# Gate half of the projection after the experts, bias and skip seeded into PSUM by ScalarE, and 64-row matmuls in pairs

## The chip, the cores and the metric

The kernel runs on one core of a Trainium2 chip. The metric is the time of one execution on the device in microseconds (us), median of several runs.

## The reference, cut to what matters

Two branches read the same layer-normed `xn` (4 sequences of 4096 tokens, 512 features, float32). The first is a recurrence over every second token, the second a mixture of experts on all tokens; their product is added to the input.

```python
xn = _layernorm(x)
# branch 1, on every second token
x_sub = xn[:, ::2]; x_sub = x_sub * rsqrt(mean(x_sub**2) + 1e-6) * g_norm
x_proj, gate = split(x_sub @ w_in.T + b_in)              # 2 x 512 columns
h = tanh(h * A + xt[:, :, None] * Bm)                    # scan over tokens, h: (4, 512, 64)
y = h @ Cm.sum(axis=0) + Dv * xt
s = repeat((y * silu(gate)) @ w_out.T + b_out, 2)
# branch 2, on all tokens
cont = sigmoid(xn @ W_enc + b_enc) @ W_s2c + b_s2c       # 512 -> 1024 -> 64
gate8 = top-2 of softmax(cont @ Wr + br), renormalised   # 8 experts
expert_out = sum_e gate8[e] * (relu(cont @ W1[e] + b1[e]) @ W2[e] + b2[e])   # 64 -> 512 -> 64
decoded = sigmoid(expert_out @ W_c2s + b_c2s) @ W_dec + b_dec                # 64 -> 1024 -> 512
g = silu(layernorm(decoded))
out = x + s * g
```

## The kernel before, in words

The 2048 steps of the recurrence are cut into 64 blocks of 32 steps; a block carries 128 kept tokens (32 steps of 4 sequences) and the 128 tokens beside them, so 256 tokens for the second branch. The state `h` lies as 128 partitions (4 sequences x 32 of the 64 states) by two halves `f` of 512 features. Of every step GpSimd makes `u = xt * B` (line 513), VectorE multiplies `h` by `A` into PSUM for both halves (line 1068) and adds `u` (line 1074), and ScalarE takes the tanh of each half (line 586). This is a loop of VectorE and ScalarE that no other engine can shorten. `h` is a ring of 8 steps. TensorE reads it four steps at a time (`y`, line 833): group `y(k)` needs the tanhs of steps 4k to 4k+3, and the tanh of step 4k+8 waits until it is done.

All other work of the block before, the block itself and the block after is woven between these steps. Each engine runs its instructions strictly in the order of hand-set "slots", the constants of lines 62 to 113: slot 10.875 of `ACT_SCALE_CONT` puts the work after the second half of step 10, slots of 32 and over fall into the next block, negative ones into the block before. TensorE has no steps of its own, so its slots give only an order. Its order in one period is: end of the experts, `y(4)`, `to_spikes` (line 954: expert output, 64 wide, to 1024 spikes; the output lies as two partial sums on 128 rows and `w_c2s` stands there twice) around `y(5)`, `decode` (971), `y(6)`, `encode` (866), `fin_transpose` (983), `controller` (878: 1024 to 64), `y(0)`, `router` (887), `fin_out` (991), `proj_transpose` (844), `y(1)`, both halves of `proj_in` (853: x_proj and gate), transposes of the scaled controller output (904), `y(2)`, and the experts (918 up, 930 down) with `y(3)` among them.

Two PSUM banks, `bank[0]` and `bank[1]`, are filled in turn by TensorE, 34 fills a block (the `FILL_` constants), and each fill waits until its bank was drained. ScalarE drains most: `spikes` (632), `contT_copy` (655), `scale_cont` (668), `relu` (685), `eo_copy` (689), the seeds of the decoder (697), `proj_evac` (622). VectorE drains `proj_in` with scale and bias (line 1083, into `xp` and `gt`), adds the skip `Dv * x` to `y` (`fin_y`, 1137), routes (1093 to 1111), scales and shifts the decoder's output (1119, 1128) and multiplies the branches (`fin_mul`, 1143, 1144). GpSimd makes the skip product (541), the gate product (546) and the last sum (555). ScalarE applies silu to `gt` in place (627).

Of the kernel before, what the change touches and what calls it, by code (L numbers as in the profile page):

```python
# [26 lines left out]
P = 128  # L27
# [29 lines left out]
FILL_ENC, FILL_FIN, FILL_XT, FILL_WIN, FILL_CONTE, FILL_W1, FILL_C2S, FILL_DEC = 0, 4, 6, 8, 10, 14, 30, 33  # L57
# [9 lines left out]
POOL_PROJ_SCALE = -22.9375  # L67
POOL_DEC_SCALE = (32.5625, 34.1875)
POOL_FIN_SKIP = 25.875
POOL_FIN_GATE = 36.0625  # L70
POOL_FIN_ADD = (49.25, 62.625)
ACT_PROJ_NORM = -23.375
ACT_PROJ_EVAC = (-23.125, -22.4375)
ACT_GATE_SILU = -5.5
ACT_SPIKES = (2.9375, 3.5, 4.625, 5.9375)
# [4 lines left out]
ACT_GATET_COPY = 13.625  # L80
# [22 lines left out]
PE_TO_SPIKES = (33.625, 34.3125, 35.9375, 36.5)  # L103
PE_DECODE = (36.625, 37.0625)
PE_FIN_TRANSPOSE = 53.0
PE_FIN_OUT = 54.4375
DVE_PROJ_EVAC = (-20.1875, -19.4375)
DVE_ROUTE = (8.5, 8.875, 9.125, 9.25, 9.25, 9.5)
DVE_ROUTE_GATE = 10.9375
DVE_DEC_SCALE = (32.75, 36.875)  # L110
DVE_DEC_SHIFT = (33.75, 37.8125)
DVE_FIN_Y = 35.75
DVE_FIN_MUL = 41.9375


def build(nc, x, w_inT, b_in, A_T, B_T, Cm, Dv, w_outT, b_out, g_norm, W_enc, b_enc, W_s2c, b_s2c,
# [12 lines left out]
    with ExitStack() as ctx:  # L129
# [70 lines left out]
        eoT = hT[:, 0, 0:T2]  # L200
        squares_p = hT[:, 0, 0:D]
# [58 lines left out]
        gate_opened = sem("gate_opened")  # L260
# [27 lines left out]
        def fill_number(blk, k):  # L288

            if isinstance(blk, int) and blk == 0:  # L290
                return 4 + k - (2 if k >= FILL_XT else 0)
            if isinstance(blk, int) and blk == LAST:
                return NFILL * blk + 2 + k - (4 if k >= FILL_CONTE else 0)
            return NFILL * blk + 2 + k
# [7 lines left out]
        def proj_fill(blk, k):  # L302

            if isinstance(blk, int) and blk == 0:
                return None, (k - FILL_XT if k < FILL_WIN else 2 + k - FILL_WIN)
            return blk - 1, k
# [75 lines left out]
        def _(sp):  # L382
# [27 lines left out]
            def store_scratch(blk, par):  # L410
                wait_drained(sp, proj_fill(blk, FILL_WIN))
# [78 lines left out]
        def _(pool):  # L490
# [748 lines left out]
```

## Time and profile before

| | |
|---|---|
| median of 3 runs | 5846.17 us (5845.11 to 5853.07) |
| the profiled execution | 5857.5 us, its span 5855.7 us |
| blocks | 64, one every 89.8 us in the middle of the span |
| busy share of the span | TensorE 96%, VectorE 95%, GpSimd 90%, ScalarE 75% |
| granted TensorE clock | 0.993 of full on the mean |

The span runs from the first to the last instruction. Busy time is the time in which an engine had at least one instruction in flight; consecutive instructions overlap a little, so that a sum of durations is more than the time they take, and start-to-start distances are used for costs. A name like `L1068` is line 1068 of the kernel.

### The profile page before, as it was taken

The page shows a single profiled execution, that of the slowest core. Times are in us where ns is not written, and L with a number is a line of the kernel's source. Part 1 is how long each engine was busy: PE and PEld are TensorE (multiplying, and loading weights), DVE is VectorE, ACT ScalarE, POOL GpSimd, SP SyncE. Part 2 cuts the span into 40 slices and gives each one's busy share as a digit, 9 for nine tenths or more (in the row PEclk, how much of TensorE's full clock was granted, in tenths as well). Part 3 has the DMA queues.
Part 4 walks back from the last instruction along what each step waited for, and adds up shares of the span by engine and source line. Part 5 has one row for each costly group of instructions (what it writes and reads, how often), then busy time and mean ns, then how long its engine had stood idle before and what let it go on. Part 6 is the DMA issues. An engine that isn't in the chain of part 4 may idle for free.

```text
span 5855.7 us, 87473 instructions
## 1 busy us (share of the span) xinstructions
PE 5645.0 (96%) x28512; PEld 3153.8 (54%) x28512; DVE 5534.8 (95%) x9300; ACT 4379.6 (75%) x9557; POOL 5298.1 (90%) x2828
## 2 busy tenths in 40 slices
PE   6999999999999999999999999999999999999998
PEld 3555555555555555555555555555555555555554
DVE  5999999999999999999999999999999999999998
ACT  5777777777777777777777777777777777777775
POOL 5999999999999999999999999999999999999897
PEclk9999999999999999999999999999999999999999
DMA  6444444444544445444444444444444444444443
GB/s 162 112 121 107 121 112 112 115 109 116 122 106 121 113 112 123 109 116 120 107 119 116 110 119 110 116 119 106 120 114 112 119 110 116 119 110 115 113 111 89
DMA packets 158218, 673.36 MB, mean 115 GB/s; under 512 B 45761, under 2 KB 46785, under 8 KB 92225
## 3 DMA queue, kind: packets, MB, share of 16 engines
q1 hardware_dynamic: 157762, 667.76, 47.5%
q8 instruction: 227, 3.72, 0.3%
q14 instruction: 229, 1.88, 0.1%
HBM read 617.26 MB, written 50.33 MB: 114 GB/s over the span
## 4 chain that ended last, share of the span: by engine, by line
PE 39%; DVE 33%; ACT 13%; issue 10%; POOL 4%; SPq 1%; DMA 0%; POOLq 0%; DVEq 0%; ACTq 0%
PE bank L918 16%; DVE ps_z L1074 15%; DVE ps_z L1068 13%; ACT h L586 8%; PE bank L853 7%; PE ps_acc L930 7%; PE ps_y L833 4%; POOL u L513 3%; PE bank L904 2%; ACT wide L632 2%; ACT xbuf L616 2%; DVE g L1128 1%; POOL p_root L518 1%; DVE gt L1083 1%; DVE g L1143 1%
## 5 line engine op out<-in xcount | busy, mean ns | idle before, releaser
L513 POOL TENSOR_TENSOR u<-xb,bt 128x1024 f32<-128x1024 f32 x2048 | 4807.9, 2366 | 479.5 <-DVE ps_z L1074 424.0
L586 ACT ACTIVATE h<-ps_z 128x512 f32<-128x512 f32 x4096 | 2421.8, 600 | 1104.8 <-DVE ps_z L1074 1087.4
L1068 DVE TENSOR_TENSOR ps_z<-h,ps_A 128x512 f32<-128x512 f32 x4096 | 2678.1, 692 | 214.3 <-ACT h L586 129.9
L1074 DVE TENSOR_TENSOR ps_z<-ps_z,u 128x512 f32<-128x512 f32 x4096 | 2660.6, 691 | 0.2 <-issue 0.2
L918 PE MATMUL bank<-wide,w 65*128 65x256 f32 x4096 | 1029.9, 396 | 0.0
L833 PE MATMUL ps_y<-h,c_wide 128*32 128x512 f32 x8192 | 978.1, 601 | 0.0
L866 PE MATMUL bank<-xnT,w_enc 128*128 128x256 f32 x4096 | 904.3, 381 | 2.9 <-ACT wide L632 2.9
L918 PEld LDWEIGHTS bank<-wide,w 65*128 65x128 f32 x4096 | 723.4, 190 | 312.0 <-issue 152.7
L866 PEld LDWEIGHTS bank<-xnT,w_enc 128*128 128x128 f32 x4096 | 775.1, 190 | 160.0 <-issue 53.3
L833 PEld LDWEIGHTS ps_y<-h,c_wide 128*32 128x32 f32 x8192 | 221.0, 109 | 515.0 <-issue 443.8
L853 PE MATMUL bank<-w_in,xnT 128*128 128x512 f32 x1024 | 452.9, 595 | 1.6 <-DVE c_wide L1160 1.6
L971 PE MATMUL bank<-w_dec,wide 128*128 128x512 f32 x1024 | 452.6, 595 | 0.0
L971 PE MATMUL ps_acc<-w_dec,wide 128*128 128x512 f32 x1024 | 449.9, 592 | 0.0
L685 ACT ACTIVATE conte<-bank 128x512 f32<-128x512 f32 x512 | 308.3, 602 | 103.0 <-PE bank L918 96.4
L685 ACT ACTIVATE hT<-bank 128x512 f32<-128x512 f32 x512 | 298.4, 597 | 89.3 <-PE bank L918 87.8
L971 PEld LDWEIGHTS ps_acc<-w_dec,wide 128*128 128x128 f32 x1024 | 194.6, 190 | 244.9 <-issue 244.9
L971 PEld LDWEIGHTS bank<-w_dec,wide 128*128 128x128 f32 x1024 | 189.0, 189 | 225.9 <-issue 166.5
L853 PEld LDWEIGHTS bank<-w_in,xnT 128*128 128x128 f32 x1024 | 190.6, 191 | 218.0 <-issue 215.9
L930 PE MATMUL ps_acc<-conte,w 128*64 128x256 f32 x2048 | 281.1, 395 | 0.0
L930 PE MATMUL ps_acc<-hT,w 128*64 128x256 f32 x2048 | 279.8, 394 | 0.0
L991 PE MATMUL bank<-w_out,conte 128*128 128x512 f32 x512 | 236.7, 605 | 19.8 <-ACT bank L710 19.8
L668 ACT ACTIVATE conte<-ps_acc,gate 128x64 f32<-128x64 f32 x1024 | 228.5, 379 | 0.0
(118 smaller groups left out, 4264.2 us busy)
## 6 DMA issues: line engine op xcount, KB each, us to landing
xb<-x_proj_scratch SPq DMA_DIRECT2D x2048, 256.0 KB, 4.5
xbuf<-in_L_attn_x SPq DMA_DIRECT2D x256, 128.0 KB
xres<-in_L_attn_x SPq DMA_DIRECT2D x512, 64.0 KB
out<-g SPq DMA_DIRECT2D x256, 128.0 KB
x_proj_scratch<-xp SPq DMA_DIRECT2D x256, 64.0 KB
w_in<-in_L_attn_w_in SPq DMA_DIRECT2D x1, 2048.0 KB, 8.3
w_enc<-in_L_ffn_W_enc SPq DMA_DIRECT2D x1, 2048.0 KB, 16.6
w_dec<-in_L_ffn_W_dec SPq DMA_DIRECT2D x1, 2048.0 KB, 20.2
```

What stands on the lines that cost most here:

```text
L513: pool.tensor_tensor(u[:, tau % 2, :, :], xt, bt[:, :, :], ALU.mult).then_inc(u_ready, 1)
L586: act.activation(h[:, tau % RING, f, :], ps_z[:, f, :], ACT.Tanh).then_inc(h_ready, 1)
L685: drained(act.activation(hidden[n % 4], bank[n % 2][:, :], ACT.Relu), at)
L833: ins = pe.matmul(ps_y[32 * j:32 * j + 32, :], c_wide[:, f, SP - 4 - 4 * k:2 * SP - 4 - 4 * k], h[:, (QUAD * k + j) % RING, f, :], start=( ...
L853: ins = pe.matmul(bank[half][:, :], xnT[:, par, k, 0, :], w_in[:, k, D * half:D * half + D], start=(k == 0), stop=(k == KD - 1))
L866: ins = pe.matmul(bank[n % 2][:, T2 * half:T2 * half + T2], w_enc[:, k, P * m:P * m + P], xnT[:, par, k, :, :], start=(k == 0 and half == ...
L918: ins = pe.matmul(bank[n % 2][:, T2 * half:T2 * half + T2], w_1[0:MA, e, P * t:P * t + P], conteT[:, e, :], start=True, stop=True)
L930: ins = pe.matmul(eo_acc[M * half:M * half + M, :], w_2[:, 4 * (n // 2) + t, :], hidden[n % 4][:, T2 * half:T2 * half + T2], start=(n == 0 ...
L971: ins = pe.matmul(dst[:, :], wide[:, k, P * q:P * q + P], w_dec[:, k, :], start=False, stop=(k == KH - 1), skip_group_check=True)
L991: ins = pe.matmul(bank[1][:, :], oT[:, k, :], w_out[:, k, :], start=False, stop=(k == KD - 1), skip_group_check=True)
L1068: dve.tensor_tensor(ps_z[:, f, :], h[:, (tau - 1) % RING, f, :], ps_A[:, f, :], ALU.mult).then_inc(m_done, 1)
L1074: dve.tensor_tensor(ps_z[:, f, :], ps_z[:, f, :], u[:, tau % 2, f, :], ALU.add).then_inc(z_ready, 1)
```

## The change

- **Gate's projection.** `proj_in` of the gate half leaves its place beside the x_proj half and runs after the experts of the block before (slot 4.625), as fill 29, ahead of the spikes' fills. The fill numbers of the expert work alternate anew, so that each bank sees the same order as before.
- **Bias by seed.** ScalarE writes `b_in` divided by the row's scale into the bank (`proj_seed`), the matmuls add onto it, and ScalarE drains with the row's scale (`proj_out`): a copy to `xp` for the first half, a silu straight into `gt` for the second. VectorE's two `proj_evac` and the silu in place are gone.
- **Skip by seed.** GpSimd multiplies `xp` by `Dv` in place once `xp` is stored (`fin_skip`, slot 0.4375, before at 25.875), ScalarE copies it into `ps_y` (`y_seed`), the `y` matmuls add onto it, and ScalarE copies the sum out (`fin_y`). VectorE's `fin_y` is gone.
- **Spikes in pairs.** Two matmuls (`eo_fold`) add the two partial sums of the expert output and put the result on both halves of the partitions; ScalarE copies it (`both_copy`); `to_spikes` then takes 64 rows for each matmul, two row halves in turn, into different banks, in two calls in place of four.
- **Controller.** `controller` waits for each pair of spike tiles before the matmuls that read it, and not for all of them first.
- The slots of all engines are set anew, and a few small operations of the scale are made in other forms.

```diff
-FILL_ENC, FILL_FIN, FILL_XT, FILL_WIN, FILL_CONTE, FILL_W1, FILL_C2S, FILL_DEC = 0, 4, 6, 8, 10, 14, 30, 33
+FILL_ENC, FILL_FIN, FILL_XT, FILL_IN, FILL_GATE, FILL_C2S, FILL_DEC = 0, 4, 6, 8, 29, 30, 33
+FILL_CONTE = (10, 9, 12, 11)
+FILL_W1 = (14, 13, 16, 15, 18, 17, 20, 19, 22, 21, 24, 23, 26, 25, 28, 27)
+FILL_WIN = (FILL_IN, FILL_GATE)
...
-POOL_PROJ_SCALE = -22.9375
-POOL_DEC_SCALE = (32.5625, 34.1875)
-POOL_FIN_SKIP = 25.875
...
-ACT_PROJ_NORM = -23.375
-ACT_PROJ_EVAC = (-23.125, -22.4375)
-ACT_GATE_SILU = -5.5
...
-ACT_CONTT_COPY = 6.6875
-ACT_ROUTE_SIG = 8.875
-ACT_SCALE_CONT = (10.875, 11.75)
-ACT_CONTET_COPY = (12.125, 12.5, 12.9375, 13.5)
...
-ACT_RELU = (13.625, 14.4375, 14.6875, 15.0, 16.75, 16.8125, 17.75, 17.8125, 18.6875, 19.6875, 19.9375, 20.0, 20.625, 21.5, 21.9375, 22.9375)
-ACT_EO_COPY = 23.6875
-ACT_SPIKES_AGAIN = (24.5, 24.9375, 26.625, 27.5625)
...
-ACT_DEC_SEED = (25.8125, 27.625)
-PE_Y = (22.3125, 22.5625, 24.0625, 26.75, 33.125, 34.375, 38.375, 45.25)
-PE_PROJ_TRANSPOSE = (-9.5625, -9.4375)
-PE_PROJ_IN = (-9.375, -9.3125)
-PE_ENCODE = (16.3125, 16.3125, 17.0, 18.4375)
-PE_CONTROLLER = 21.8125
-PE_ROUTER = 22.3125
-PE_CONTET = (22.8125, 23.75, 23.875, 24.6875)
-PE_GATET = 24.5625
-PE_EXPERTS = (25.125, 25.125, 26.3125, 27.5625, 28.4375, 29.0625, 30.0, 30.3125, 32.0)
...
-DVE_PROJ_EVAC = (-20.1875, -19.4375)
-DVE_ROUTE = (8.5, 8.875, 9.125, 9.25, 9.25, 9.5)
...
-DVE_FIN_Y = 35.75
...
+POOL_FIN_SKIP = 0.4375
...
+ACT_PROJ_NORM = -23.4375
+ACT_PROJ_EVAC = (-22.6875, -20.25)
+ACT_PROJ_SEED = (-22.3125, -9.125)
+ACT_PROJ_OUT = (-20.4375, -7.25)
+ACT_FIN_Y = 33.8125
+ACT_Y_SEED = 5.625
+ACT_SPIKES = (2.9375, 3.8125, 4.6875, 5.875)
+ACT_CONTT_COPY = 6.8125
+ACT_ROUTE_SIG = 9.5
...
+ACT_RELU = (13.375, 13.875, 14.5625, 14.75, 15.5, 15.5625, 16.5625, 16.5625, 17.8125, 17.8125, 18.8125, 20.9375, 21.625, 21.875, 22.6875, 22.8125)
+ACT_EO_COPY = 23.625
+ACT_BOTH_COPY = 24.875
+ACT_SPIKES_AGAIN = (25.75, 25.9375, 26.625, 27.75)
...
+ACT_DEC_SEED = (26.3125, 27.875)
+PE_Y = (19.1875, 20.375, 21.5, 34.8125, 34.9375, 37.25, 38.125, 38.375)
+PE_PROJ_TRANSPOSE = (-12.0, -10.625)
+PE_PROJ_IN = (-11.5625, 4.625)
+PE_ENCODE = (6.4375, 7.1875, 7.3125, 11.1875)
+PE_CONTROLLER = 17.125
+PE_ROUTER = 19.0625
+PE_CONTET = (22.0, 26.3125, 27.4375, 28.0)
+PE_GATET = 21.4375
+PE_EXPERTS = (28.9375, 33.3125, 34.0, 34.125, 34.4375, 34.4375, 35.5625, 35.9375, 36.25)
...
+PE_EO_FOLD = 36.75
+PE_TO_SPIKES = (36.9375, 37.3125)
+PE_DECODE = (37.4375, 37.8125)
...
+PE_FIN_TRANSPOSE = 50.8125
+PE_FIN_OUT = 51.25
...
+DVE_ROUTE = (7.75, 8.75, 9.375, 9.5, 9.625, 9.75)
+DVE_ROUTE_GATE = 10.0
...
@@ -257,7 +266,10 @@
         p_moments = sem("p_moments")
         p_scale_steps = sem("p_scale_steps")
         p_normed = sem("p_normed")
-        gate_opened = sem("gate_opened")
+        proj_seeded = sem("proj_seeded")
+        y_seeded = sem("y_seeded")
+        eo_folded = sem("eo_folded")
+        both_copied = sem("both_copied")
         contT_ready = sem("contT_ready")
         contT_copied = sem("contT_copied")
...
@@ -515,13 +527,13 @@
             def proj_scale(blk):
 
                 pool.wait_ge(p_moments, blk + 1)
-                pool.tensor_tensor(p_root[:, :, :], p_var[:, :, :], minus_half[:, :].rearrange("p (n q) -> p n q", n=2),
-                                   ALU.pow).then_inc(p_scale_steps, 1)
+                pool.tensor_tensor(p_root[:, 0:3], p_var[:, 0:3], minus_half[:, 0:3], ALU.pow).then_inc(p_scale_steps, 1)
                 pool.wait_ge(p_scale_steps, 4 * blk + 1)
-                pool.tensor_tensor(p_nm[:, :], p_mean[:, :], p_root[:, 0, :], ALU.mult).then_inc(p_scale_steps, 1)
-                pool.tensor_tensor(p_rr[:, :], p_var[:, 0, :], p_root[:, 0, :], ALU.mult).then_inc(p_scale_steps, 1)
+                pool.tensor_tensor(p_nm[:, :], p_mean[:, :], p_root[:, 0:2], ALU.mult).then_inc(p_scale_steps, 1)
+                pool.tensor_tensor(p_both[:, :], p_root[:, 0:1], p_root[:, 2:3], ALU.mult).then_inc(p_scale_steps, 1)
                 pool.wait_ge(p_scale_steps, 4 * blk + 3)
-                pool.tensor_tensor(p_rr[:, :], p_rr[:, :], p_root[:, 1, :], ALU.mult).then_inc(p_scale_steps, 1)
+                pool.tensor_tensor(p_rr[:, :], p_var[:, 0:4:2], p_both[:, :].to_broadcast([P, 2]),
+                                   ALU.mult).then_inc(p_scale_steps, 1)
 
...
                     pool.wait_ge(late_loaded, LATE)
-                pool.wait_ge(eo_ready, blk + 1)
-                pool.tensor_tensor(o, xp[:, par, :], dv_all[:, :], ALU.mult).then_inc(t1_ready, 1)
+                pool.wait_ge(scratch_stored, 16 * QUAD * (blk + 1))
+                pool.tensor_tensor(xp[:, par, :], xp[:, par, :], dv_all[:, :], ALU.mult).then_inc(t1_ready, 1)
 
             def fin_gate(blk, par):
-                pool.wait_ge(gate_opened, blk + 1)
+                wait_drained(pool, proj_fill(blk, FILL_GATE))
                 pool.wait_ge(y_taken, blk + 1)
                 pool.tensor_tensor(o, o, gt[:, par, :], ALU.mult).then_inc(o_ready, 1)
...
                 drained(act.activation(xnT[:, par, :, q, :],
                                        bank[q][:, :].rearrange("p (k t) -> p k t", k=KD), ACT.Copy), at)
 
-            def gate_silu(blk, par):
-                wait_drained(act, proj_fill(blk, FILL_WIN + 1))
-                act.activation(gt[:, par, :], gt[:, par, :], ACT.Silu).then_inc(gate_opened, 1)
+            def proj_seed(blk, half):
+
+                wait_free(act, proj_fill(blk, FILL_WIN[half]))
+                act.wait_ge(p_scale_steps, 4 * blk + 4)
+                act.activation(bank[half][:, :], b_in_all[:, D * half:D * half + D], ACT.Copy,
+                               scale=p_rr[:, 1:2]).then_inc(proj_seeded, 1)
+
+            def proj_out(blk, par, half):
+
+                at = proj_fill(blk, FILL_WIN[half])
+                wait_filled(act, at)
+                if half == 0:
+                    if not (is_first(blk) or blk == 1):
+                        act.wait_ge(y_seeded, blk - 1)
+                    ins = act.activation(xp[:, par, :], bank[0][:, :], ACT.Copy, scale=p_rr[:, 0:1])
+                else:
+                    ins = act.activation(gt[:, par, :], bank[1][:, :], ACT.Silu, scale=p_rr[:, 0:1])
+                drained(ins, at)
+
+            def y_seed(blk, par):
+
+                act.wait_ge(t1_ready, blk + 1)
+                if not is_first(blk):
+                    act.wait_ge(y_taken, blk)
+                act.activation(ps_y[:, :], xp[:, par, :], ACT.Copy).then_inc(y_seeded, 1)
+
+            def fin_y(blk):
+
+                act.wait_ge(y_done, NQ * (blk + 1))
+                act.activation(o, ps_y[:, :], ACT.Copy).then_inc(y_taken, 1)
 
             def half_tanhs(src, k, bias):
...
                 act.activation(eoT, eo_acc, ACT.Copy).then_inc(eo_copied, 1)
+
+            def both_copy(blk):
+                act.wait_ge(eo_folded, blk + 1)
+                act.activation(eoT_both, eo_acc, ACT.Copy).then_inc(both_copied, 1)
 
             def dec_seed(blk, q):
...
@@ -824,16 +880,14 @@
             def y(blk, k):
 
                 pe.wait_ge(h_ready, 2 * STEPS * blk + 2 * QUAD * (k + 1))
-                if k == 0 and is_first(blk):
-                    pe.wait_ge(biases_shifted, 2)
-                elif k == 0:
-                    pe.wait_ge(y_taken, blk)
+                if k == 0:
+                    pe.wait_ge(y_seeded, blk + 1)
                 for f in range(F):
                     for j in range(QUAD):
                         ins = pe.matmul(ps_y[32 * j:32 * j + 32, :],
                                         c_wide[:, f, SP - 4 - 4 * k:2 * SP - 4 - 4 * k],
                                         h[:, (QUAD * k + j) % RING, f, :],
-                                        start=(k == 0 and f == 0), stop=(k == NQ - 1 and f == F - 1))
+                                        start=False, stop=(k == NQ - 1 and f == F - 1), skip_group_check=True)
                 ins.then_inc(y_done, 1)
 
...
             def proj_in(blk, par, half):
 
-                at = proj_fill(blk, FILL_WIN + half)
+                at = proj_fill(blk, FILL_WIN[half])
                 wait_drained(pe, proj_fill(blk, FILL_XT))
-                wait_free(pe, at)
+                pe.wait_ge(proj_seeded, 2 * blk + half + 1)
                 for k in range(KD):
                     ins = pe.matmul(bank[half][:, :], xnT[:, par, k, 0, :], w_in[:, k, D * half:D * half + D],
-                                    start=(k == 0), stop=(k == KD - 1))
+                                    start=False, stop=(k == KD - 1), skip_group_check=True)
                 filled(ins, at)
 
...
             def controller(blk):
 
-                wait_drained(pe, (blk, FILL_ENC + 2))
-                wait_drained(pe, (blk, FILL_ENC + 3))
                 pe.wait_ge(acc_seeded, blk + 1)
                 for k in range(KH):
                     half = k % 2
+                    if half == 0:
+                        wait_drained(pe, (blk, FILL_ENC + k // 2))
                     ins = pe.matmul(contT_acc[M * half:M * half + M, :], w_s2c[:, k, :], wide[:, k, :],
...
@@ -895,7 +950,7 @@
                 ins.then_inc(gateT_ready, 1)
 
             def conteT_transpose(blk, n):
-                at = (blk, FILL_CONTE + n)
+                at = (blk, FILL_CONTE[n])
                 pe.wait_ge(conte_ready, 2 * blk + 2)
                 wait_free(pe, at)
...
@@ -942,21 +997,32 @@
                     expert_down(blk, 2 * p - 2)
                     expert_down(blk, 2 * p - 1)
 
+            def eo_fold(blk):
+
+                pe.wait_ge(eo_copied, blk + 1)
+                for j in range(2):
+                    ins = pe.matmul(eo_acc[M * j:M * j + M, :], halves, eoT, start=True, stop=True)
+                ins.then_inc(eo_folded, 1)
+
             def to_spikes(blk, n):
+
                 if n == 0:
-                    pe.wait_ge(eo_copied, blk + 1)
-                at = None if C2S_FILL[n] is None else (blk, C2S_FILL[n])
-                if at:
-                    wait_free(pe, at)
-                dst = bank[at[1] % 2] if at else ps_acc
+                    pe.wait_ge(both_copied, blk + 1)
+                ats = [None if C2S_FILL[2 * n + j] is None else (blk, C2S_FILL[2 * n + j]) for j in range(2)]
+                for at in ats:
+                    if at:
+                        wait_free(pe, at)
                 for half in range(2):
-                    m = 2 * n + half
-                    ins = pe.matmul(dst[:, T2 * half:T2 * half + T2], w_c2s[:, P * m:P * m + P],
-                                    eoT, start=(half == 0), stop=True, skip_group_check=True)
-                if at:
-                    filled(ins, at)
-                else:
-                    ins.then_inc(acc_filled, 1)
+                    for j in range(2):
+                        dst = bank[ats[j][1] % 2] if ats[j] else ps_acc
+                        m = 2 * (2 * n + j) + half
+                        rows = slice(M * j, M * j + M)
+                        ins = pe.matmul(dst[:, T2 * half:T2 * half + T2], w_c2s[rows, P * m:P * m + P],
+                                        eoT_both[rows, :], start=(half == 0), stop=True, skip_group_check=True)
+                        if half == 1 and ats[j]:
+                            filled(ins, ats[j])
+                        elif half == 1:
+                            ins.then_inc(acc_filled, 1)
 
             def decode(blk, q):
...
@@ -1073,17 +1143,6 @@
                     dve.wait_ge(m_done, t2 + f + 1)
                     dve.tensor_tensor(ps_z[:, f, :], ps_z[:, f, :], u[:, tau % 2, f, :],
                                       ALU.add).then_inc(z_ready, 1)
-
-            def proj_evac(blk, par, half):
-
-                at = proj_fill(blk, FILL_WIN + half)
-                wait_filled(dve, at)
-                dve.wait_ge(p_scale_steps, 4 * blk + 4)
-                dst = (xp, gt)[half]
-                drained(dve.scalar_tensor_tensor(out=dst[:, par, :], in0=bank[half][:, :], scalar=p_rr[:, 0:1],
-                                                 in1=b_in_all[:, D * half:D * half + D],
-                                                 op0=ALU.mult, op1=ALU.add), at)
-
 
             def route(blk, n):
...
@@ -1131,11 +1190,6 @@
                 else:
                     ins.then_inc(acc_drained, 1)
 
-            def fin_y(blk):
-                dve.wait_ge(t1_ready, blk + 1)
-                dve.wait_ge(y_done, NQ * (blk + 1))
-                dve.tensor_tensor(o, ps_y[:, :], o, ALU.add).then_inc(y_taken, 1)
-
             def fin_mul(blk):
```

## Rows read from the trace of the kernel before

**Rows 1.** The page: span, engines, chain that ended last, the recurrence's multiplies.

```profile
span 5855.7 us, 87473 instructions
PE 5645.0 (96%) x28512; PEld 3153.8 (54%) x28512; DVE 5534.8 (95%) x9300; ACT 4379.6 (75%) x9557; POOL 5298.1 (90%) x2828
...
PE 39%; DVE 33%; ACT 13%; issue 10%; POOL 4%; SPq 1%; DMA 0%; POOLq 0%; DVEq 0%; ACTq 0%
...
L1068 DVE TENSOR_TENSOR ps_z<-h,ps_A 128x512 f32<-128x512 f32 x4096 | 2678.1, 692 | 214.3 <-ACT h L586 129.9
```

**Rows 2.** Windows, one period and ten: length, busy PE to POOL, clock, DMA.

```profile
3011.95:3101.75 89.80, 87.57 (x448) 48.99 (x446) 86.30 (x146) 68.24 (x150) 82.79 (x45) 1.00 0.47 115
1000.00:1898.00 898.00, 875.76 (x4427) 489.05 (x4425) 857.97 (x1442) 678.46 (x1478) 824.18 (x439) 0.99 0.48 114
```

**Rows 3.** Timeline of VectorE: start, length, line, tiles, count, [idle before].

```profile
3014.51 1.30 DVE L1068 TENSOR_TENSOR ps_z<-h,ps_A 128x512 f32<-128x512 f32 x2
...
3017.07 1.30 DVE L1068 TENSOR_TENSOR ps_z<-h,ps_A 128x512 f32<-128x512 f32 x2
...
3043.62 1.30 DVE L1068 TENSOR_TENSOR ps_z<-h,ps_A 128x512 f32<-128x512 f32 x2
...
3046.03 0.68 DVE L1137 TENSOR_TENSOR conte<-ps_y,conte 128x512 f32<-128x512 f32 x1
3046.63 1.28 DVE L1068 TENSOR_TENSOR ps_z<-h,ps_A 128x512 f32<-128x512 f32 x2
...
3070.81 1.28 DVE L1068 TENSOR_TENSOR ps_z<-h,ps_A 128x512 f32<-128x512 f32 x2
3072.00 0.69 DVE L1074 TENSOR_TENSOR ps_z<-ps_z,u 128x512 f32<-128x512 f32 x1
3072.96 0.75 DVE L1083 SCALAR_TENSOR_TENSOR gt<-bank,p_rr,b_in_all 128x512 f32<-128x512 f32 x1 [0.27 <-PE bank L853]
...
3074.23 1.45 DVE L1068 TENSOR_TENSOR ps_z<-h,ps_A 128x512 f32<-128x512 f32 x2
```

**Rows 4.** Timeline of TensorE's matmuls, the same period, columns as there.

```profile
3015.40 1.99 PE L954 MATMUL bank<-hT,w_c2s 128*128 128x256 f32 x8
3017.32 1.92 PE L833 MATMUL ps_y<-h,c_wide 128*32 128x512 f32 x16
3019.18 1.13 PE L954 MATMUL ps_acc<-hT,w_c2s 128*128 128x256 f32 x4
...
3021.01 7.07 PE L971 MATMUL bank<-w_dec,wide 128*128 128x512 f32 x16
...
3034.88 3.64 PE L833 MATMUL ps_y<-h,c_wide 128*32 128x512 f32 x32
3038.45 14.08 PE L866 MATMUL bank<-xnT,w_enc 128*128 128x256 f32 x64
...
3054.24 1.95 PE L878 MATMUL ps_acc<-wide,w_s2c 128*64 128x256 f32 x16 [1.28 <-ACT wide L632]
...
3073.86 1.06 PE L904 MATMUL bank<-ident,conte 128*65 128x128 f32 x8 [0.39 <-DVE gt L1083]
...
3082.85 1.99 PE L918 MATMUL bank<-wide,w 65*128 65x256 f32 x8
3084.77 1.08 PE L930 MATMUL ps_acc<-conte,w 128*64 128x256 f32 x8
3085.78 1.93 PE L833 MATMUL ps_y<-h,c_wide 128*32 128x512 f32 x16
```

**Rows 5.** Timeline of ScalarE, three steps, columns as there.

```profile
3016.44 1.20 ACT L586 ACTIVATE h<-ps_z 128x512 f32<-128x512 f32 x2 [1.09 <-DVE ps_z L1074]
3017.53 1.56 ACT L632 ACTIVATE wide<-bank,b_c2s_col 128x256 f32<-128x256 f32 x4
...
3029.24 1.20 ACT L586 ACTIVATE h<-ps_z 128x512 f32<-128x512 f32 x2 [1.36 <-DVE ps_z L1074]
```

**Rows 6.** Groups by line: the expert output's copy; busy us, mean ns.

```profile
L689 ACT ACTIVATE hT<-ps_acc 128x256 f32<-128x256 f32 x64 | 24.2, 377 | 0.0
```

More of the change, by code:

```diff
@@ new lines @@
+ACT_CONTET_COPY = (12.625, 12.75, 12.75, 12.9375)
+ACT_GATET_COPY = 11.6875
+ACT_RELU = (13.375, 13.875, 14.5625, 14.75, 15.5, 15.5625, 16.5625, 16.5625, 17.8125, 17.8125, 18.8125, 20.9375, 21.625, 21.875, 22.6875, 22.8125)
+ACT_EO_COPY = 23.625
+ACT_BOTH_COPY = 24.875
+ACT_SPIKES_AGAIN = (25.75, 25.9375, 26.625, 27.75)
+ACT_DEC_SILU = (31.5, 39.9375)
+ACT_DEC_SQUARE = (29.9375, 31.625)
+ACT_PROJ_SUM = (-29.25, -29.0625)
+ACT_PROJ_MEAN = -28.9375
+ACT_PROJ_SQUARE = (-28.0625, -27.375)
+ACT_PROJ_VAR = -25.0625
@@ new lines @@
+ACT_FIN_EVAC = 39.875
+ACT_ACC_SEED = 5.625
+ACT_OUT_SEED = 38.9375
+ACT_DEC_SEED = (26.3125, 27.875)
[9 more added lines that the diff above has]
+PE_EO_FOLD = 36.75
@@ L200, in build @@
         eoT = hT[:, 0, 0:T2]
+        eoT_both = hT[:, 0, T2:2 * T2]
+        halves = w_r[:, E * E:E * E + M]
         squares_p = hT[:, 0, 0:D]
@@ L292, in fill_number @@
             if isinstance(blk, int) and blk == LAST:
-                return NFILL * blk + 2 + k - (4 if k >= FILL_CONTE else 0)
+                return NFILL * blk + 2 + k - (2 if k > FILL_XT + 1 else 0) - (2 if k > FILL_GATE or k % 2 == 0 and k > FILL_IN else 0)
             return NFILL * blk + 2 + k
@@ L739, in _ @@
             proj_evac(0, 0, 0)
+            proj_seed(0, 0)
             proj_evac(0, 0, 1)
+            proj_seed(0, 1)
+            proj_out(0, 0, 0)
             act.wait_ge(early_loaded, EARLY)
@@ L761, in _ @@
             act.wait_ge(acc_shaped, 1)
+            proj_out(0, 0, 1)
             def between(blk, par, slot):
@@ L778, in between @@
                     proj_var(blk)
-                if slot == ACT_GATE_SILU:
-                    gate_silu(blk, par)
+                for half in range(2):
+                    if slot == ACT_PROJ_SEED[half]:
+                        proj_seed(blk, half)
+                for half in range(2):
+                    if slot == ACT_PROJ_OUT[half]:
+                        proj_out(blk, par, half)
+                if slot == ACT_FIN_Y:
+                    fin_y(blk)
+                if slot == ACT_Y_SEED:
+                    y_seed(blk, par)
                 for k in range(4):
@@ L800, in between @@
                     eo_copy(blk)
+                if slot == ACT_BOTH_COPY:
+                    both_copy(blk)
                 for k in range(4):
@@ L918, in expert_up @@
                     ins = pe.matmul(bank[n % 2][:, T2 * half:T2 * half + T2], w_1[0:MA, e, P * t:P * t + P],
[L919 removed]
+                                    conteT[:, e, :], start=(half == 0), stop=True, skip_group_check=True)
                 filled(ins, at)
@@ L1009, in _ @@
             proj_in(0, 0, 0)
-            proj_in(0, 0, 1)
             pe.wait_ge(weights_shaped, 3)
+            zeros = h[:, RING - 1, 0, :]
+            pe.matmul(ps_y[:, :], zeros[:, 0:P], zeros, start=True, stop=True)
             for k in range(KH):
-                pe.matmul(ps_y[0:M, 0:1], w_s2c[:, k, :], ones[:, 0:1], start=(k == 0), stop=(k == KH - 1))
+                pe.matmul(ps_y[0:M, 0:1], w_s2c[:, k, :], ones[:, 0:1], start=False, stop=(k == KH - 1),
+                          skip_group_check=True)
             for k in range(KH):
@@ L1042, in between @@
                         experts(blk, n)
-                for n in range(4):
+                if slot == PE_EO_FOLD:
+                    eo_fold(blk)
+                for n in range(2):
                     if slot == PE_TO_SPIKES[n]:
@@ L1185, in between @@
             def between(blk, par, slot):
-                for half in range(2):
-                    if slot == DVE_PROJ_EVAC[half]:
-                        proj_evac(blk, par, half)
                 for n in range(6):
@@ L1198, in between @@
                         dec_shift(blk, q)
-                if slot == DVE_FIN_Y:
-                    fin_y(blk)
                 if slot == DVE_FIN_MUL:
```

63 lines of the change are left out of this document (24 added, 39 removed).

## The prediction

> **What bounds the kernel now.** I read the page first, for who is busy at all. TensorE has 96% and VectorE 95% of the span, GpSimd 90%, ScalarE 75%, and the chain that ended last is 39% TensorE and 33% VectorE [rows 1]. So there are two candidates, and neither alone need be the bound. The windows come next, because the kernel repeats itself 64 times: one period takes 89.80 us, and in it TensorE is busy for 87.57, VectorE for 86.30, GpSimd for 82.79 and ScalarE for 68.24. Ten periods give the same shares [rows 2]. The reader should see that TensorE has 2.23 us left in a period.
>
> VectorE's timeline shows what its 86.30 are. A plain step of the recurrence goes from 3014.51 to 3017.07, 2.56 us, four operations and a hand-over to ScalarE and back [rows 3]. 32 of these are 81.9 us, and so 7.9 us of each period are steps made longer, by an operation of VectorE between them or by a tanh that comes late. The second kind costs 129.9 us in all, 2.0 in a period [rows 1]. ScalarE's timeline shows why it can be late: in a plain step it does two tanhs in 1.20 us and is then idle for 1.36, which holds two operations of 512 columns (0.60 each, half of the 1.20) and not three [rows 5]. So TensorE's stream and the loop of VectorE with ScalarE each run at about 98% of the period, tied to each other through the banks, the relus and the ring of `h`. Only a change that takes time from both shortens the period.
>
> **The change part by part.** All sums are for one period, against the profiled execution's own 89.80 us. That execution took 5857.5 us, 11 more than the median of 5846.2, so differences are carried over to the median.
>
> *VectorE.* It loses `fin_y`: the step with it goes from 3043.62 to 3046.63, 3.01 us, 0.45 more than a plain one [rows 3]. It loses the drain of x_proj, an operation of the same kind (0.45), and the drain of the gate half: the step with it goes from 3070.81 to 3074.23, 3.42 us, 0.86 more, of which 0.27 are a wait for the matmuls [rows 3]. Nothing is added. The loop comes to 89.80 - 0.45 - 0.45 - 0.86 = 88.04, if ScalarE is as late as before and not later.
>
> *ScalarE.* It gains two bias seeds, the copy to `xp`, the seed and the drain of `ps_y`, each about 0.60 [rows 5], and `both_copy` at 0.38 as its twin `eo_copy` has [rows 6]; the silu is only moved. That is 3.4 us, and 68.2 + 3.4 = 71.6 of some 88. The free gaps of 32 steps are 32 x 1.36 = 43.5 us, and ScalarE's work beside the tanhs is now 68.2 - 32 x 1.20 = 29.8, after it 33.2. So it fits on the mean, at nothing. If the cover is missing, each operation that is a third one in its gap delays the step by up to 0.5; some places have that (silu, then `both_copy`, just ahead of step 25's tanh; two relus and a seed ahead of step 23). The new waits on ScalarE are for the gate's matmuls before `proj_out`, for the fold before `both_copy`, for the last `y` before `fin_y`, and for GpSimd's product before `y_seed`. The tanhs are queued behind all four, and VectorE waits for the tanhs. By their slots the first two are the ones that matter; the other two have most of a step or more to spare.
>
> *TensorE's work.* `to_spikes` takes 3017.32 - 3015.40 = 1.92 and 3021.01 - 3019.18 = 1.83, together 3.75 us for 16 instructions [rows 4]. The trace has no pair of row halves, but a pair of column halves: eight instructions of line 930, as many columns, take 3085.78 - 3084.77 = 1.01, against 3084.77 - 3082.85 = 1.92 for eight unpaired of line 918 [rows 4]. The bounds for the sixteen are these two paces, 2.02 and 3.75. I take 2.02, because line 930 is the same array cut in half in the other direction. `eo_fold` has four instructions of line 930's form, 0.50. `y(3)` and `y(4)` now stand side by side; 32 such instructions take 3.57 where 16 take 1.86 [rows 4], so this saves 0.15. The work is 87.57 - 3.75 + 2.02 + 0.50 - 0.15 = 86.19.
>
> The 0.15 is also the only price here of changing how the array is cut. The Trainium skill (TensorEngine Tiling (Array Packing), Key Properties) says that changing the tiling mode, not just the tile, drains TensorE, which speaks against this change: around the spikes it has seven such changes where there were five. The trace bears it out at about 0.15 for two changes, one into `y` and one out of it, and the two that `y(4)` no longer needs pay for the new ones, so by the rule the sum stays as it is.
>
> *TensorE's waits.* They are 89.80 - 87.57 = 2.23 now. The wait of the controller for the last spikes is 1.28 [rows 4]. After the change its first 12 of 16 matmuls run ahead of those spikes, 12/16 of the 1.95 us of the row, that is 1.4; but `fin_transpose`, 0.6 us of cover, now stands behind it. 1.28 + 0.6 - 1.4 leaves 0.45, a gain of 0.83. The 0.39 behind the drain of the gate half [rows 4] go, since the drain is off this path. The router now has only `fin_transpose` between it and the controller whose output ScalarE must copy first, where `y(0)` stood, 1.86: the copy (0.38, as in rows 6) and two hand-overs, for which I take 0.25 each as a guess between 0 and 0.5, are about 0.9, less 0.6 of cover, so 0.3; the bounds are 0 and 1.5, with a pair of tanhs in front. The worst new wait is behind the fold: `eo_copy` is hidden behind the gate's matmuls, but after the fold nothing stands between it and `to_spikes`. ScalarE first does the silu (0.60, half of it during the fold), then `both_copy` (0.38), with hand-overs about 1.0. The bounds are 0.7 and 2.2, the upper one with a pair of tanhs in front (1.20) [rows 5]. The seed of the gate half stands behind the last relu, as the last pair of expert matmuls does on TensorE, and both take about as long; I put it at 0, at most 0.6. The waits come to 2.23 - 0.83 - 0.39 + 0.3 + 1.0 = 2.31.
>
> *GpSimd.* The same product is made earlier, in place, with 1.3 us of work moved into the first step and a reciprocal root over three columns in place of four. 82.8 of 88 remain busy; `u` is made up to two steps ahead. I put it at 0; it costs up to 0.5 if `u` comes late in step 1. *SyncE's* queue has the same transfers at the same slots. *The head and the tail* of the span change by less than I can tell.
>
> **Sum.** TensorE's stream is 86.19 + 2.31 = 88.5, the loop of the recurrence 88.04. The larger sets the period: 88.5, a gain of 1.3, and 64 x 1.3 = 83 us. 5846.2 - 83 = 5763 us. Its own range, from the bounds of the waits (period 87.6 to 89.4), is 5705 to 5821.
>
> **The rivals.**
> 1. *Both streams lose their losses.* With less on both sides the late tanhs (2.0) and TensorE's waits may shrink too. TensorE's work is 86.2; with waits of 0.8 the period is 87.0, 64 x 2.8 = 179, 5667 us. For it: every wait of TensorE but the one behind the fold has a cover. Against it: the coupling that makes late tanhs (relus at TensorE's pace of 2.93 us a pair against steps of 2.56) stays.
> 2. *The paired rows do not overlap.* Then the spikes stay at 3.75, and TensorE's stream is 88.5 + 1.73 = 90.2, of which perhaps 0.3 are given back, since the wait behind the fold then has less after it to delay: about 90.0, 13 us more, 5859 us. For it: no row of the trace shows row halves, and the two halves in turn write different banks but through the same columns. Against it: the column pairs of line 930. The Trainium skill (TensorEngine Tiling (Array Packing), Gotcha 1) has row tiles write to different PSUM banks, as the change does; no row here shows that.
> 3. *Slower: ScalarE becomes the late one.* Place: slots 22.7 to 24.9, where seed, silu and `both_copy` join the relus and copies, and where ScalarE stands waiting for the gate's matmuls and then the fold with a tanh behind. Price: six added operations, each the third in its gap, 6 x 0.4 = 2.4 (three operations, 1.80, against the gap of 1.36), plus about 1.0 of standing in the two waits: 88.04 + 3.4 = 91.4, 64 x 1.6 = 102, 5948 us. It decides from 1.8 us of added lateness on (89.80 - 88.04). For it: the gaps hold two operations, and two now come just ahead of a tanh. Against it: ScalarE has 10 us more gap than work.
> 4. *No effect.* The gains are eaten in part, by late tanhs or by a `y` that waits for the ring since TensorE's order around it is new. Period 89.8, 5846 us.
>
> **How the numbers follow.** The forecast has 0.52, rival 1 0.13, rival 2 0.10, rival 3 0.17, rival 4 0.08. The range takes in the forecast's own, most of rival 1 and rivals 2 and 4, and the near part of 3: 5670 to 5880. A measurement of this kernel can tell about 0.2%, 12 us, from no change. Faster: 0.52 + 0.13 and half of what lies around rivals 2 and 4 on that side (0.05), 0.70. Same: 0.09. Slower: 0.17 + 0.04 = 0.21.
>
> **What the profile of after would show.** Right: VectorE's busy time per period near 84.5; eight instructions of `to_spikes` in about 1.0 us; a gap of about 1 us before the first of them; the controller's wait under 0.5; late tanhs still near 2 us a period. Wrong: eight instructions in 1.9 (rival 2); VectorE's idle time before its multiplies, put down to the tanh, over 240 us in all (rival 3); a period below 87.3 (rival 1). What would undo the forecast most easily is the stretch around the fold, where TensorE and ScalarE wait for each other in turn.

## The result, and the profile after

The changed kernel takes 5802.8 us (median of 5 runs, 5799.2 to 5817.2), the kernel before 5853.1 beside it (5 runs); the ratio is 0.9919, with a 95% interval of 0.9896 to 0.9942. That is 50 us less by the medians and 47 by the ratio, which compares the means. It lies inside the range, at a bit over half of the 83 us forecast. The page of the changed kernel (busy times and the chain that ended last, to be held against rows 1), and the window of one period (length, busy times of PE, PEld, DVE, ACT, POOL, granted clock, DMA; against rows 2):

```profile
span 5801.0 us, 88242 instructions
PE 5580.6 (96%) x28770; PEld 3073.1 (53%) x28770; DVE 5403.5 (93%) x9108; ACT 4595.4 (79%) x9941; POOL 5287.9 (91%) x2828
...
PE 76%; ACT 14%; DVE 7%; issue 3%; SPq 1%; DMA 0%; POOL 0%; ACTq 0%; POOLq 0%
...
3009.36:3098.52 89.16, 86.79 (x449) 47.83 (x448) 84.24 (x143) 71.59 (x156) 82.59 (x45) 1.00 0.47 115
```

Work has left VectorE (86.30 to 84.24 in a period) and gone to ScalarE (68.24 to 71.59), as the sum had it. The chain is what changed most: 76% TensorE and 7% VectorE, where it was 39% and 33% [rows 1]. TensorE's timeline over that period, main rows (start, length, line, tiles, count, idle before):

```profile
3012.93 14.08 PE L921 MATMUL bank<-xnT,w_enc 128*128 128x256 f32 x64
3026.95 1.95 PE L933 MATMUL ps_acc<-wide,w_s2c 128*64 128x256 f32 x16
3028.83 0.66 PE L1049 MATMUL bank<-ident,conte 128*128 128x128 f32 x4
3029.38 0.71 PE L942 MATMUL ps_acc<-w_r,hT 128*128 128x128 f32 x4
...
3038.16 3.67 PE L908 MATMUL bank<-w_in,xnT 128*128 128x512 f32 x8
3041.67 0.60 PE L898 MATMUL bank<-ident,xbuf 128*128 128x128 f32 x4
3042.53 0.38 PE L949 MATMUL ps_acc<-ident,gate 128*8 128x128 f32 x2 [0.26 <-ACT conte L707]
3043.69 1.92 PE L887 MATMUL ps_y<-h,c_wide 128*32 128x512 f32 x16 [0.78 <-ACT h L598]
...
3046.97 1.11 PE L959 MATMUL bank<-ident,conte 128*65 128x128 f32 x8 [0.34 <-ACT wide L718]
3048.37 3.90 PE L973 MATMUL bank<-wide,w 65*128 65x256 f32 x16 [0.29 <-ACT wide L718]
...
3075.84 3.70 PE L908 MATMUL bank<-w_in,xnT 128*128 128x512 f32 x8
3079.47 0.65 PE L1004 MATMUL ps_acc<-hT,w_r 128*64 128x256 f32 x4
3080.61 1.14 PE L1020 MATMUL bank<-hT,w_c2s 64*128 64x256 f32 x8 [0.48 <-ACT hT L732]
3081.67 1.92 PE L887 MATMUL ps_y<-h,c_wide 128*32 128x512 f32 x16
```

The controller (L933) and the router (L942) no longer wait at all; the pairs (L1020) take 3081.67 - 3080.61 = 1.06 us for eight. New are a row of four waits around `y(2)`, the third `y` after the encoder, 0.26, 0.78, 0.34 and 0.29, together 1.67, and 0.48 behind the fold. From start to start of the same operations, one period divides so:

| stage on TensorE | before, us | after, us |
|---|---|---|
| y(6), y(7) | 3.57 | 3.57 |
| encoder, up to the controller | 15.79 | 14.02 |
| controller to fin_out | 4.74 | 5.12 |
| fin_out to the first expert | 18.38 | 16.30 |
| experts, up to their end | 25.97 | 27.47 |
| to the decoder (spikes; after: gate, fold, spikes) | 7.49 | 8.75 |
| decoder | 13.87 | 13.93 |
| sum | 89.81 | 89.16 |

The first gain is the controller's wait and `fin_transpose` (which moved one stage on). The fourth stage lost the gate half, about 3.5, and the waits of 0.39 and 0.20 for VectorE, which would make 14.3; it takes 16.3. There the gain was given back.

In both kernels `y(6)` and `y(7)` stand back to back ahead of the encoder. The starts of this doubled `y`, 63 in each trace, give the account of nearly the whole span. Before, 59 of the 62 periods take 89.8 to 89.9 us and three 94.7; after, all 62 take 89.17. In the three long ones the granted clock of TensorE was at half, 1.2 of 2.4 GHz, for some 10 us, as these windows of the kernel before show (length, busy times of PE, PEld, DVE, ACT, POOL, granted clock, DMA share, GB/s):

```profile
1000.00:1011.00 11.00, 10.61 (x58) 5.79 (x56) 10.06 (x17) 9.89 (x25) 8.82 (x4) 1.00 0.24 60
1011.00:1021.60 10.60, 10.60 (x43) 4.71 (x42) 8.85 (x15) 4.83 (x9) 9.55 (x6) 0.53 0.35 71
```

So 64 x (89.80 - 89.17) = 40 and 3 x 4.9 = 15, together 55, which is the difference of the two spans (5855.7 - 5801.0). Between these two executions a quarter of the gain is clock that was no longer lost, and the sum had no term for it. The steady part, 40 us, is a little under half of the 83 forecast.

### The profile page after: what moved, and what is told of

Read it like the earlier page. It is cut to its first block, busy times and chain, and to the rows that moved or that the text cites. A ratio compares the mean times of both kernels' runs of the same rounds, so it can differ in the third digit from the quotient of the medians.

```text
span 5801.0 us, 88242 instructions
## 1 busy us (share of the span) xinstructions
PE 5580.6 (96%) x28770; PEld 3073.1 (53%) x28770; DVE 5403.5 (93%) x9108; ACT 4595.4 (79%) x9941; POOL 5287.9 (91%) x2828
## 3 DMA queue, kind: packets, MB, share of 16 engines
q8 instruction: 229, 3.75, 0.3%
## 4 chain that ended last, share of the span: by engine, by line
PE 76%; ACT 14%; DVE 7%; issue 3%; SPq 1%; DMA 0%; POOL 0%; ACTq 0%; POOLq 0%
PE bank L973 17%; PE bank L921 15%; PE ps_y L887 11%; PE ps_acc L985 9%; PE bank L1037 8%; PE ps_acc L1037 8%; ACT h L598 4%; PE bank L908 4%; DVE ps_z L1144 4%; ACT conte L707 3%; DVE ps_z L1138 2%; ACT wide L718 1%; PE bank L1020 1%; PE ps_acc L1020 1%; PE bank L959 1%
## 5 line engine op out<-in xcount | busy, mean ns | idle before, releaser
L973 PE MATMUL bank<-wide,w 65*128 65x256 f32 x4096 | 1015.0, 393 | 18.5 <-ACT wide L718 18.5
L887 PE MATMUL ps_y<-h,c_wide 128*32 128x512 f32 x8192 | 962.0, 599 | 49.0 <-ACT h L598 49.0
L887 PEld LDWEIGHTS ps_y<-h,c_wide 128*32 128x32 f32 x8192 | 227.2, 109 | 566.8 <-issue 418.1
L908 PE MATMUL bank<-w_in,xnT 128*128 128x512 f32 x1024 | 474.4, 606 | 7.6 <-DVE c_wide L1214 1.6
L724 ACT ACTIVATE conte<-bank 128x512 f32<-128x512 f32 x512 | 291.2, 598 | 24.3 <-PE bank L973 24.3
```

The lines of the kernel that those rows point to most:

```text
L724: drained(act.activation(hidden[n % 4], bank[n % 2][:, :], ACT.Relu), at)
L887: ins = pe.matmul(ps_y[32 * j:32 * j + 32, :], c_wide[:, f, SP - 4 - 4 * k:2 * SP - 4 - 4 * k], h[:, (QUAD * k + j) % RING, f, :], start=F ...
L908: ins = pe.matmul(bank[half][:, :], xnT[:, par, k, 0, :], w_in[:, k, D * half:D * half + D], start=False, stop=(k == KD - 1), skip_group_c ...
L973: ins = pe.matmul(bank[n % 2][:, T2 * half:T2 * half + T2], w_1[0:MA, e, P * t:P * t + P], conteT[:, e, :], start=(half == 0), stop=True, ...
```

## The experiments

All kernels below were timed beside the kernel before; their times are held against 5803 of the changed kernel, "steady period" is the commonest distance between the starts of the doubled `y`. The kernel before had medians of 5856.8, 5857.7 and 5867.3 us in the three rounds of experiments, against 5853.1 beside the changed kernel, so a difference from 5803 is uncertain by up to some 14 us. The steady periods carry the readings.

### Do row halves overlap?

```diff
-                        rows = slice(M * j, M * j + M)
+                        rows = slice(0, M)
```

> The changed kernel, but both matmuls of a pair read rows 0 to 63 instead of one reading 0 to 63 and the other 64 to 127; the same 16 instructions, the same data (it lies on both halves), nothing left out. Theory A (row halves overlap, and TensorE's stream sets the period): eight instructions take about 1.9 us in place of 1.06, twice a period, so 1.7 x 64 = 109 us more than the changed kernel's 5803, about 5912. Rival B (row halves do not overlap, 1.06 is something else): 1.06 stays, 5803. Rival C (they overlap, but the recurrence's loop on VectorE and ScalarE sets the period): eight instructions take 1.9, the time stays within 15 us of 5803.

5914.2 us, ratio 1.0095 (1.008 to 1.011), steady period 90.88.

```profile
3047.40 1.99 PE L1020 MATMUL bank<-hT,w_c2s 64*128 64x256 f32 x8 [0.48 <-ACT hT L732]
3049.32 1.92 PE L887 MATMUL ps_y<-h,c_wide 128*32 128x512 f32 x16
```

Eight matmuls on one row half take 3049.32 - 3047.40 = 1.92 us, on two in turn 1.06. Theory A is right to 2 us: rows overlap, and 1.71 us of TensorE in a period cost 1.71 x 64. In this stretch the stream of TensorE sets the time.

### The spikes as before, in the changed kernel

```diff
-                if slot == ACT_BOTH_COPY:
-                    both_copy(blk)
...
-                    pe.wait_ge(both_copied, blk + 1)
+                    pe.wait_ge(eo_copied, blk + 1)
...
-                        rows = slice(M * j, M * j + M)
+                        rows = slice(0, P)
...
-                                        eoT_both[rows, :], start=(half == 0), ...)
+                                        eoT[rows, :], start=(half == 0), ...)
...
-                if slot == PE_EO_FOLD:
-                    eo_fold(blk)
```

> The changed kernel with the spikes as before: no fold, no second copy, 16 matmuls over 128 rows, in the two calls of the changed kernel. The rest of the change stays. Theory A (TensorE's stream sets the period): the spikes go from 2.12 + 0.66 for the fold + 0.48 of waiting to 3.75, so +0.5 x 64 = 32 us, about 5835. Rival C (the recurrence's loop sets it): ScalarE loses a copy and a wait, 5803 or a little under, 5790.

5887.1 us, ratio 1.0048 (1.0033 to 1.0063): 84 more, where A had 32.

```profile
3037.05 1.97 PE L1018 MATMUL bank<-hT,w_c2s 128*128 128x256 f32 x8 [0.87 <-ACT gt L653]
```

The direction was right and a term was missing: the first spikes go into the bank that the silu drains, and without the fold before them they wait 0.87 us for it. The steady period is 90.47, and 1.30 x 64 = 83. So the fold and its wait cost less than the sum had, since most of that time would otherwise be waiting for the silu.

### The controller all at once, and in pieces in the kernel before

```diff
+                wait_drained(pe, (blk, FILL_ENC + 2))
+                wait_drained(pe, (blk, FILL_ENC + 3))
...
-                    if half == 0:
-                        wait_drained(pe, (blk, FILL_ENC + k // 2))
```

> The changed kernel, but the controller waits for the last two pairs of spike tiles before its first matmul, as in the kernel before. Theory A: 12 of its 16 matmuls no longer run ahead of the last tanhs; a wait of about 1.4 us stands before it in each period, and router, routing and the scaled controller output all come that much later: 64 x 1.4 = 90 us more, about 5890. Rival C: TensorE's wait is covered by the slack of its stream, within 15 us of 5803.

5858.9 us, ratio 1.0002 (0.9993 to 1.0012), steady period 90.00. The wait is 0.98 us, not 1.4; 0.83 of it reach the period, 53 us. (The profiled execution has two periods of 103.1 us besides, with the clock at half for 27 us; more on these below.) The same edit the other way round, in the kernel before:

> The kernel before with one part of the change alone: the controller waits for each pair of spike tiles before the matmuls that read it. In the changed kernel the same edit was worth 56 us when taken away. Theory D (the period is a path in series, on TensorE from the relus to the encoder in the changed kernel, but only between slots 11 and 23 in the kernel before, whose controller stands in the stretch paced by the recurrence): TensorE's wait of 1.28 goes from the controller to the next thing that waits for the recurrence, the time stays, ratio 0.998 to 1.001. If TensorE's stream set the period all along: 0.9 x 64 = 56 us less, ratio 0.990.

5855.3 us beside 5867.3, ratio 0.9980 (0.9971 to 0.9989), steady period 89.80, exactly that of before.

```profile
3061.46 1.95 PE L878 MATMUL ps_acc<-wide,w_s2c 128*64 128x256 f32 x16 [0.47 <-ACT ps_acc L703]
...
3067.00 3.67 PE L991 MATMUL bank<-w_out,conte 128*128 128x512 f32 x8 [0.97 <-ACT bank L710]
```

The controller's wait falls from 1.28 [rows 4] to 0.47, and `fin_out`'s grows from 0.29 to 0.97. One edit is worth 0.83 us a period in one kernel and nothing in the other, since before it stood in a stretch paced by the recurrence. The ratio's 0.2% (12 us) has no steady gain behind it. It goes with the clock: the mean granted clock was 0.992 to 0.996 in the runs of this kernel and 0.990 to 0.993 in those of the kernel before beside it.

### One slot moved

```diff
-PE_Y = (19.1875, 20.375, 21.5, 34.8125, ...
+PE_Y = (19.1875, 20.375, 22.5, 34.8125, ...
```

> The changed kernel with one slot moved: y(2) from 21.5 to 22.5 in TensorE's order, so behind the first four transposes of the scaled controller output and not ahead of them. In the trace of the changed kernel TensorE stands 0.78 us waiting for the tanhs that y(2) reads, while the transposes could already run. Theory A (that wait is on the path that sets the period): four transposes, about 0.6 us, go into it, and the relus start earlier: 64 x 0.5 = 32 us less than 5803, about 5770. Rival C: nothing, 5803.

5861.2 us, ratio 1.0007 (0.9997 to 1.0016): 58 more, where theory A had 32 less.

```profile
3076.46 0.62 PE L959 MATMUL bank<-ident,conte 128*65 128x128 f32 x4 [1.45 <-ACT xp L651]
3077.01 3.62 PE L887 MATMUL ps_y<-h,c_wide 128*32 128x512 f32 x16
```

I had missed a wait: the transposes go into the bank that `proj_out` drains to `xp`, and on ScalarE that copy is behind the same tanh. The 0.78 became 1.45, and 0.31 of it reach the steady period (89.48). In 24 of the 62 periods, as here, `y(2)` then ran at half clock, 3.62 us, and these periods took 91.1: 24 x 1.64 = 39 us, about two thirds of the 58. A wait in the trace names only what came last: the transposes had a second thing to wait for, just as late.

### VectorE's work given back, and one operation in four places

```diff
+                if slot in (3.75, 11.8125, 12.5625):
+                    dve.tensor_reduce(spare[:, :], ln_g_all[:, :], AX.X, ALU.add)
```

> The changed kernel with three more operations of VectorE in each block, a sum over 512 columns into one spare column, at slots 3.75, 11.8 and 12.6, where the kernel before has fin_y and the two drains of the projection. It gives VectorE back the work that the change took from it; nothing else changes. Theory A (TensorE's stream sets the period, the recurrence only in slots 6 to 11): two of the three lie where the recurrence has slack, and the first where ScalarE is the later one; within 12 us of the changed kernel's 5803. Rival C (the loop of VectorE and ScalarE sets the period): 3 x 0.45 x 64 = 86 us more, about 5889.

5975.1 us, ratio 1.0196 (1.0173 to 1.022): 172 more. Both theories miss it. The steady period is 90.53, 1.36 more than 89.17, which is 3 x 0.45 and 87 us: rival C's price. The rest is TensorE's clock. Windows just ahead of and in one such fall, and the waits ahead of it:

```profile
540.00:564.00 24.00, 21.34 (x116) 10.62 (x114) 22.19 (x44) 21.04 (x54) 20.85 (x13) 1.00 0.39 93
564.00:592.00 28.00, 28.00 (x91) 14.88 (x94) 15.42 (x25) 11.35 (x21) 16.46 (x7) 0.51 0.32 70
...
554.76 1.92 PE L888 MATMUL ps_y<-h,c_wide 128*32 128x512 f32 x16 [0.78 <-ACT h L599]
...
558.91 1.11 PE L960 MATMUL bank<-ident,conte 128*65 128x128 f32 x8 [1.20 <-ACT wide L719]
```

The transposes' wait for ScalarE's copies grew from 0.34 to 1.20, and in six of the periods the clock was at half afterwards, twice for 27 us and four times for 34, which made those periods 13 and 16 us longer: 2 x 13.1 + 4 x 16.1 = 91 us of the profiled execution, which took 176 more than that of the changed kernel. The single operations:

> The changed kernel with one such operation of VectorE in each block, at slot 8.25. In the trace of the changed kernel y(2) waits 0.78 us for the tanh of step 11, and TensorE's path goes on from there. Theory A: the recurrence is on the path between slots 6 and 11 only, so this one operation costs its full 0.45 x 64 = 29 us, about 5832. If nowhere on VectorE is on the path: 5803.

5836.2 us, ratio 0.9975 (0.9963 to 0.9987), steady period 89.66, so +0.49: its full price, as said. The profiled execution has one long period, 102.7 us, with the clock at half for 27.

> The changed kernel with one such operation of VectorE in each block, at slot 26.75, in the recurrence's steps beside the decoder. ScalarE waits 1.1 us for y(6) a few steps later in the changed kernel, so there is slack. Theory A: 5803, within 12. Rival C: 29 us more, 5832.

5804.4 us, ratio 0.9914 (0.9899 to 0.9929), steady period 89.17: nothing, as said.

> The kernel before with one such operation of VectorE in each block at the same slot 26.75. Its chain of waits runs over VectorE and ScalarE from slot 23 to slot 10. Theory A': in the kernel before this stretch is on the path, so 0.45 to 0.5 x 64 = 29 to 32 us more than before, a ratio of 1.005. If TensorE's stream set the period there as well: ratio 1.000 to 1.001.

Ratio 1.0086 (1.0066 to 1.0106), 5900.4 beside 5857.7: above both figures that were expected. The steady period is 90.2, +0.4 and 26 us, near the first of them; the profiled execution has ten periods with the clock at half in place of three, 7 x 4.9 = 34 us more. So the same operation at the same slot costs its price before and nothing after.

> The changed kernel with one more operation of VectorE in each block, at slot 12.56, one of the three that together cost 172 us. Theory D: it delays the tanh of step 12, the copies of the transposed controller output stand behind that tanh on ScalarE, and TensorE waits for them: 0.86 us in each period, 55 us, and TensorE's granted clock falls to half now and then behind that longer row of waits, as in the run with three; with a few such stretches 5860 to 5910. If the 172 us were an even price of three operations: 57 us, 5860, and no fall of the clock beyond the one of the changed kernel.

5841.7 us, ratio 0.9949 (0.9932 to 0.9966), steady period 89.61, +0.44. The transposes' wait:

```profile
3064.81 1.11 PE L960 MATMUL bank<-ident,conte 128*65 128x128 f32 x8 [0.78 <-ACT wide L719]
```

I had 0.86, for all of the longer wait, but about half of it (0.34 to 0.78) is this operation's, and both forecasts, some 5860, were too high. One period shows the clock at half, again for 27 us. So a single operation brings the fall once in the profiled execution here and at slot 8.25, and three together bring it six times; the changed kernel with its controller held back had it twice without any added operation.

### One copy more on ScalarE

```diff
+                if slot == 24.8125:
+                    act.activation(b_dec_all[:, :], b_dec_all[:, :], ACT.Copy)
```

> The changed kernel with one more copy of 512 columns on ScalarE in each block, at slot 24.81, between the silu of the gate and the copy behind the fold. Theory D: TensorE stands waiting for that copy, so all of its 0.50 is on the path: 32 us, 5835. If the time of ScalarE were covered there: 5803.

> The same copy on ScalarE at slot 30.56, beside the decoder, where ScalarE is idle for 1.36 us of each step. Theory D: no cost, 5803 within 10.

5834.8 us at slot 24.81 (ratio 0.9951, 0.9936 to 0.9966; steady period 89.68, +0.51) and 5806.2 at 30.56 (ratio 0.9899, 0.9884 to 0.9914; steady period 89.17). Both as said: the copy is free in the gap at 30.56, and costs its full 0.50 where TensorE stands waiting behind it.

## Why the prediction was right in its direction and high in its size

**Spikes in pairs.** Right. The pace of the column pairs carried over, 1.06 against 1.01, and the first experiment shows the overlap. The fold took 3080.61 - 3079.47 less 0.48 of waiting, 0.66 against 0.50.

**The wait behind the fold** was put at 1.0 and is 0.48: the silu starts during the fold. **Controller and router** were put at 0.45 and 0.3 and are 0 and 0.

**TensorE's work** was put at 86.19 and is 86.79 busy. The period was put at 88.5 and is 89.17, so in the sum's own terms nearly all of the miss, 0.60 of 0.67, stands here. Most of it has rows: the projection in two parts takes 3.51 and 3.63 where it took 6.93 in one (+0.21), the fold (+0.16) and the pairs (+0.10).

**The step that failed** is the list of TensorE's waits. Its total was 2.31 and the measured one is 2.37, but that is luck: it was too high by 0.45, 0.3 and 0.52 in the three terms above, and it kept two old waits that went (0.29 at `fin_out`, 0.20 at the second transpose); on the other side are the four new ones, 1.67 us around `y(2)`, of which it had none. The measured gain came as near to the forecast as it did by a second piece of luck, the 15 us of clock. The controller starts earlier, the gate half is gone from between, and so TensorE arrives at the transposes before ScalarE has scaled the controller's output and at `y(2)` before the tanh of step 11. The prediction asked what covers each new wait and not who is late when TensorE comes early.

**Two streams, and the larger sets the period**: this form of the sum was wrong. The two are in series. Operations of VectorE at slots 3.75 to 12.6 cost 0.44 to 0.49 each in the changed kernel, though TensorE's own stream, by the sum, was the longer one, and one at 26.75 costs nothing; matmuls cost their full time at the spikes (the first experiment). That they would at the relus and in the decoder too is read from the chain and was not tried. Before, the recurrence's part of the path ran from slot 23 to slot 10 by the chain of waits, and two runs bear on it (one operation at 26.75: +0.4, a controller without its wait: 0). The change handed most of it to TensorE. VectorE's relief was put at 1.76, of which 0.27 were a wait; three operations given back, without such a wait, cost 1.36, since they lie where the recurrence still is on the path. With them the changed kernel takes 90.53 a period, 0.73 more than before. So all the rest of the change together costs 0.73, though the pairs (1.30) and the controller in pieces (0.83) are part of it. If these prices add, which was not tried, the remainder costs nearly 3 us. How that divides among seeds, gate and slots was not tried either.

**ScalarE** (rival 3) did not decide, but the tanhs came late more often: the idle time that VectorE's multiplies lay behind them grew from 129.9 [rows 1] to this, just under the 240 that was set as the sign; it is 3.6 a period where about 2 was expected to stay:

```profile
L1138 DVE TENSOR_TENSOR ps_z<-h,ps_A 128x512 f32<-128x512 f32 x4096 | 2664.7, 691 | 314.7 <-ACT h L598 233.1
```

In part this is no loss, since where TensorE sets the pace the tanh itself waits for `y(3)` and `y(6)`: ScalarE's idle time ahead of tanhs put down to `y` (L887) is 173.9 us in all.

**GpSimd** at nothing was right: its 82.59 did not show in the chain.

## What to carry to other kernels

Where two nearly full engines are tied by waits, ask of each part of the period which of them is on the path there; a gain counts only in its own part, and the next wait downstream takes the rest. To learn it, put one cheap operation more at two or three places and time it: here that cost 0.4 to 0.5 us a period, or nothing. When an engine will come earlier to a point, list everything it meets there, the bank's drain too, and not only the wait it leaves behind.

## What was unexpected of the hardware

TensorE's granted clock fell to 1.2 GHz inside a kernel that keeps it 96% busy, and stayed there for 3 to 34 us at a time. A fall cost 1.6 us where the one `y(2)` ran at half clock (3 us), 4.9 in the kernel before (10 us), and 13 to 16 in the longest (27 and 34 us). What TensorE did before a fall differed: one wait of 1.45 us just ahead with `y(2)` moved, 2.7 us idle in 24 with the longest wait 1.20 in the case shown, and only 0.29, 0.20 and 0.39 in the 24 us ahead of the falls in the kernel before.

The same waits stood in every period, and only some periods had a fall. Between head and tail of the span, where every run has some, there were three before, none in the changed kernel, six with three operations given back, ten in the kernel before with one operation more and 24 with `y(2)` moved. They are not scattered: the ten came in exactly every sixth period, 546.1 us apart, and the 24 mostly in every second or third. What sets this rhythm is left open. So up to two thirds of a measured difference was clock, and the difference of two medians is the price of an edit only after the steady periods have been compared.
